# One ring of PSUM banks for projections and MLP, with squares and rotation taken from the bank and Newton steps on GpSimd

## The chip, the core and the metric

The kernel runs on one core of a Trainium2 chip. A core has TensorE (PE in the profile; its weight loads are PEld), VectorE (DVE), ScalarE (ACT), GpSimd (POOL) and SyncE (SP), which issues most DMAs. Matrix results land in eight PSUM banks of 128 partitions x 512 f32; DVE and ACT read these banks. Each engine works through its own list of instructions in program order and waits on semaphores. The metric is the device time of one execution in microseconds (us); lower is better.

## What is computed

Eight samples of 1024 tokens x 256 channels go through an attention block (first stage) and then through two layers of a local transformer. What matters here is one such layer:

```python
def _layer(x, wqkv, qs, ksc, wo, lg, lb, w1, b1, w2, b2):
    h = shift_token(x)              # half of the channels one token late
    q, k, v = jnp.split(h @ wqkv, 3, axis=-1)      # 8 heads of 64
    q = l2norm(q) * qs
    k = l2norm(k) * ksc
    q, k = rotary_xpos(q, k)        # x * cos + rotate_half(x) * sin
    o = local_attention(q, k, v)    # windows of 128, each sees itself and the one before
    x = x + o @ wo
    h = shift_token(x)
    mu = h.mean(-1, keepdims=True)
    var = h.var(-1, keepdims=True)
    h = (h - mu) / jnp.sqrt(var + 1e-05) * lg + lb
    a, g = jnp.split(h @ w1 + b1, 2, axis=-1)
    h = a * jax.nn.gelu(g, approximate=False)
    return x + h @ w2 + b2
```

## The kernel before, in words

After the modulation and the attention stage come two calls of `layer_stage`, one for each layer (names with the prefix b_ in the profile). Each runs a hardware loop over the eight samples and then a short closing part. The work of one sample is laid out in steps `pp` from -6 to 36. Scores are computed at steps 0 to 31, one pair of heads per step, so 4 steps make a window of 128 rows and 8 windows a sample. Every engine runs the same list of steps, each with its own pieces of a step in the order in which its code names them; no scheduler intervenes. Lines are those of the kernel before.

**A window's queries and keys.** Six steps ahead of a window's first scores TensorE projects its queries (L1573, 128x512, six matmuls), five ahead its keys, and at its first step its values; all three go through bank p. Matrices are kept as a high and a low part, and three products stand for one. ACT copies q and k into SBUF (`b_qk`, L1442) and squares both in one instruction; DVE sums the squares (L1732) and clips the sums (L1733); ACT seeds the inverse root by a logarithm and an exponential; DVE refines it with Newton steps (L114 `b_inv`) and scales the q part (L1759). DVE also multiplies q and k by the cosine table in one instruction (L1743, 128x1024) and by the sine table in two (L1749). GpSimd adds the halves (L1352, two instructions) and scales k by its inverse norms (L1358). TensorE turns q and k (L1606, bank t); ACT takes the high parts, DVE the low parts (`b_q_lo` L1784, `b_k_lo` L1790).

**Attention.** Per step: scores (L1620, banks s0 and s1), masked row maxima on DVE (L1775), exponentials on ACT (L1470), shares on DVE (L1795) that GpSimd multiplies in (L1367), the turn of the weights (L1632, bank et), the meeting with the values (L1645, bank ot). Once a window: the copy of the turned weights on DVE (L1802), `b_o_lo` (L1816), the output projection (L1573 into bank t) and its addition to the rows (`add_attention`).

**MLP.** Four units of 256 tokens; three have their statistics at steps 13, 21 and 29 (`plan_mlp`), the last one of a sample runs ahead of the next sample's first step (u = -1, from step -6). Per unit: row statistics on DVE (L1835), variance, the seed of its root on ACT and Newton steps on DVE (L114 `b_rstd`), the normalised rows, their turn and scaling (hT), six pieces `ag` one step after hT (TensorE 128x256, then gelu on ACT, then a multiplication by DVE, L1871), the product's low part on GpSimd (L1384), w2 and the store. hT, ag and w2 alternate between banks m0 and m1. GpSimd makes the low part of hT (L1373) and adds b2 (L1378). Before the first gelu of a unit ACT loads its table (L1495).

**What sets the order of banks.** `plan_fills` lists for each bank what fills it in which turn; a fill waits until the turn before it in the same bank has been read. Banks before: p, t, s0, s1, et, ot, m0, m1.

## Time and profile before

| | us |
|---|---|
| Three runs | 5864.05, 5875.67, 5878.0 (median 5875.67) |
| The profiled execution's own time | 5885.19 |
| Its span | 5883.4 |
| Mean granted clock of TensorE, share of full | 0.888 |

Busy time over the whole span: PE 4514.8 us (77%), weight loads 3167.8 (54%), DVE 3568.6 (61%), ACT 2631.7 (45%), POOL 1731.0 (29%). The attention stage ends at about 2040 us; the rest are the two layer stages, about 229 us for a sample of the first layer and 233 for one of the second. The page's own chain of waits is made of short pieces (15% of it is "issue", 8% POOL, 7% PE), so the page says what is busy but not what decides; the timeline of one sample does. In a timeline a row is: start, duration, engine, line, operation, output <- inputs, shapes, and in brackets the idle time before it with what ended it.

### The profile page before, as it was taken

The page shows a single profiled execution, that of the slowest core. Times are in us where ns is not written, and L with a number is a line of the kernel's source. Part 1 is how long each engine was busy: PE and PEld are TensorE (multiplying, and loading weights), DVE is VectorE, ACT ScalarE, POOL GpSimd, SP SyncE. Part 2 cuts the span into 40 slices and gives each one's busy share as a digit, 9 for nine tenths or more (in the row PEclk, how much of TensorE's full clock was granted, in tenths as well). Part 3 has the DMA queues.
Part 4 walks back from the last instruction along what each step waited for, and adds up shares of the span by engine and source line. Part 5 has one row for each costly group of instructions (what it writes and reads, how often), then busy time and mean ns, then how long its engine had stood idle before and what let it go on. Part 6 is the DMA issues. An engine that isn't in the chain of part 4 may idle for free. (4 is left out here: it accounts for less than half of the span.)

```text
span 5883.4 us, 97285 instructions
## 1 busy us (share of the span) xinstructions
PE 4514.8 (77%) x31439; PEld 3167.8 (54%) x31439; DVE 3568.6 (61%) x8906; ACT 2631.7 (45%) x5436; POOL 1731.0 (29%) x1344
## 2 busy tenths in 40 slices
PE   3778777777787577887877887857788787887886
PEld 1333433333333266666666666646666666666665
DVE  3666666656666565665755755736565575575664
ACT  1434334334343254554544544535454454454543
POOL 1010110101101133433433433424343443343443
PEclk6889898989898789999988989979899898898988
DMA  4132242242222500000000000010000000000000
GB/s 93 41 79 44 57 99 45 57 73 62 65 54 55 109 15 14 13 11 15 12 13 15 10 13 17 10 55 14 20 16 15 20 15 20 20 14 18 16 15 21
DMA packets 177374, 202.00 MB, mean 34 GB/s; under 512 B 32479, under 2 KB 131259, under 8 KB 176707
## 3 DMA queue, kind: packets, MB, share of 16 engines
q1 hardware_dynamic: 176806, 194.81, 14.2%
q8 instruction: 309, 5.06, 0.4%
q14 instruction: 259, 2.12, 0.1%
HBM read 123.12 MB, written 63.25 MB: 32 GB/s over the span
## 5 line engine op out<-in xcount | busy, mean ns | idle before, releaser
L858 DVE TENSOR_REDUCE a_mx<-a_unit 128x1 f32<-128x512 f32 (+3 forms) x1584 | 817.6, 553 | 434.6 <-PE a_unit L677 303.9
L582 ACT ACTIVATE a_e_t<-a_ring 128x1024 f32<-128x1024 f32 (+3 forms) x768 | 615.4, 810 | 957.6 <-PE a_ring L702 735.8
L1367 POOL TENSOR_TENSOR b_e<-b_e,b_share 128x512 f32<-128x512 f32 (+1 forms) x512 | 527.5, 1030 | 1293.7 <-DVE b_share L1795 1293.7
L1470 ACT ACTIVATE b_e<-b_e,b_bias 128x256 f32<-128x256 f32 (+1 forms) x1024 | 498.6, 488 | 615.1 <-DVE b_bias L1775 614.0
L673 PE MATMUL a_unit<-a_k_st,a_q_st 96*128 96x512 bf16 (+3 forms) x1584 | 535.0, 345 | 206.9 <-DVE a_mx L858 167.6
L699 PE MATMUL a_ring<-a_q_st,a_k_st 99*128 99x512 bf16 (+3 forms) x1536 | 529.4, 358 | 167.0 <-DMA a_q_st<-maxima 89.9
L1573 PE MATMUL b_bank_m<-b_h_t_hi,b_w_hi 128*128 128x256 f32 x1584 | 476.0, 301 | 94.0 <-POOL b_h_t_lo L1373 71.9
L1573 PE MATMUL b_bank_p<-b_wqkv_hi,b_turned_hi 128*128 128x512 f32 x768 | 373.6, 486 | 182.5 <-ACT b_qk L1442 140.1
L673 PEld LDWEIGHTS a_unit<-a_k_st,a_q_st 96*128 96x128 bf16 x1584 | 154.4, 100 | 598.3 <-DVE a_mx L858 473.5
L1573 PE MATMUL b_bank_m<-b_h_t_lo,b_w_hi 128*128 128x256 f32 x1584 | 461.3, 291 | 0.0
L1573 PE MATMUL b_bank_m<-b_h_t_hi,b_w_lo 128*128 128x256 f32 x1584 | 460.6, 291 | 0.0
L1871 DVE SCALAR_TENSOR_TENSOR b_ag<-b_bank_m,b_b_c,b_ag 128x256 f32<-128x256 f32 x396 | 191.5, 484 | 398.4 <-ACT b_ag L1498 393.6
L1775 DVE CUSTOM_DVE_ANT_0 b_e<-b_bank_s,b_mask,b_scale_q 128x256 f32<-128x256 f32 (+1 forms) x1024 | 432.2, 460 | 0.0
L1632 PE MATMUL b_bank_et<-b_ident,b_e 128*128 128x128 f32 x1920 | 352.5, 309 | 39.5 <-ACT b_e_t L1551 36.0
L1573 PEld LDWEIGHTS b_bank_m<-b_h_t_hi,b_w_hi 128*128 128x128 f32 x1584 | 317.9, 201 | 109.6 <-POOL b_h_t_lo L1373 77.9
L1498 ACT ACTIVATE b_ag<-b_bank_m,b_b_c 128x256 f32<-128x256 f32 x396 | 187.8, 474 | 402.7 <-PE b_bank_m L1573 400.2
L514 POOL TENSOR_TENSOR a_x<-a_x,a_xl 128x1024 f32<-128x1024 f32 x16 | 37.7, 2355 | 1084.6 <-DVE a_xl L962 1084.6
L1645 PE MATMUL b_bank_ot<-b_e_t,b_v 128*64 128x128 f32 x3840 | 356.2, 306 | 0.0
L718 PE MATMUL a_outp<-a_e_t,a_v_t 128*32 128x512 f32 (+3 forms) x3072 | 352.8, 533 | 0.0
L1620 PE MATMUL b_bank_s<-b_k_hi,b_q_hi 64*128 64x256 f32 (+1 forms) x1024 | 204.5, 390 | 176.1 <-DVE b_bias L1775 121.6
L699 PEld LDWEIGHTS a_ring<-a_q_st,a_k_st 99*128 99x128 bf16 x1536 | 160.0, 104 | 328.3 <-issue 264.2
L1573 PE MATMUL b_bank_p<-b_wqkv_hi,b_turned_lo 128*128 128x512 f32 x768 | 336.4, 438 | 0.0
(217 smaller groups left out, 11767.5 us busy)
## 6 DMA issues: line engine op xcount, KB each, us to landing
a_q_st<-parts_q SPq DMA_DIRECT2D x216, 128.0 KB, 7.3
a_k_st<-parts_k SPq DMA_DIRECT2D x216, 128.0 KB, 9.7
b_fl<-f_rows SPq DMA_DIRECT2D x72, 256.0 KB, 4.0
parts_q<-a_qk_part SPq DMA_DIRECT2D x18, 768.0 KB, 3.5
parts_k<-a_qk_part SPq DMA_DIRECT2D x18, 768.0 KB, 3.8
a_xl<-in_L_attn_x SPq DMA_DIRECT2D x9, 1024.0 KB, 8.9
f_rows<-b_fr SPq DMA_DIRECT2D x33, 256.0 KB, 2.1
b_x_l<-x_rows SPq DMA_DIRECT2D x33, 256.0 KB, 3.1
```

The source lines that it names most:

```text
L582: act.activation(e_t[:, step % 2, 2 * pair:2 * pair + 2, 0:cols], slot[:, :].rearrange("p (h t) -> p h t", h=2)[:, :, 0:cols], ACT.Exp).th ...
L673: mm = pe.matmul(slot[:, 0:cols], q_st[0:KROWS, head, t * P:(t + 1) * P], k_st[0:KROWS, head, 512 * piece:512 * piece + cols], start=True, ...
L699: mm = pe.matmul(slot[:, 512 * hh:512 * hh + cols], k_st[:, head, s * P:(s + 1) * P], q_st[:, head, lo:lo + cols], start=True, stop=not di ...
L718: mm = pe.matmul(outp[32 * h:32 * h + VW, lo:512], v_t[:, s, 4 * g + h, :], e_t[:, (g * NSTEP + n) % 2, h, 0:512 - lo], start=(s == 0), st ...
L858: dve.reduce_max(mx[:, h, col:col + 1], slot[:, 0:cols], AX.X).then_inc(read.sem, 1)
L1367: pool.tensor_tensor(weights, weights, share[:, pp, :].unsqueeze(2) .broadcast_to([P, 2, 2 * WIN - lo]), ALU.mult).then_inc(e_done.sem, 1)
L1470: ins = act.activation(weights, weights, ACT.Exp, scale=-1.0, bias=bias[:, pp, hh:hh + 1], accum_out=total[:, pp, hh:hh + 1])
L1573: mm = pe.matmul(out, lhs(a), rhs(b), start=(first and j == 0), stop=(last and j == 2))
L1620: mm = pe.matmul(slot[:, lo:2 * WIN], q_p[a][rows, w % 2, p, :], k_p[b][rows, p, key_slots(w), :], start=(j == 0), stop=(j == 2))
L1632: mm = pe.transpose(slot[:, at:at + WIN], e[:, pp % E_RING, hh, b * WIN:(b + 1) * WIN], ident[:, :])
L1645: mm = pe.matmul(bank["ot"][D2 * hh:D2 * (hh + 1), p * WIN:(p + 1) * WIN], v[:, u % 3, 2 * p + hh, :], e_t[:, pp % 2, 2 * hh + b, :], star ...
L1775: dve.tensor_tensor_reduce(out=e[:, pp % E_RING, hh, lo:], in0=src[:, lo:2 * WIN], in1=mask[:, int(w > 0 and w % K_RING == 0), lo:], scale ...
```

## The change

The two banks m0 and m1 and the bank p become a ring of three, r0 to r2, in which q, k, v, hT, ag and w2 follow one another in the order of the steps. v is projected one step later (step 1 of the window), w2 of every unit at s + 6 (before: s + 5, and s + 6 for u = -1). Queries are turned at step -3 (before -2), keys at -2 (before -1). For the closing part, where there are no projections, `CLOSING_AT` counts the fills apart.

ACT squares q and k straight from the ring's bank, in two instructions of 128x512 with one operand in PSUM, and copies neither. DVE multiplies by cosine and sine straight from the bank (L1800 and L1805 of the kernel after, 128x512 each, four per window): q's two in the last step of a window, k's two in the first step of the next, where k's are interleaved with the MLP's first multiplications. The bank comes free with the sine product. The clip of the sums, the Newton steps for the norms and for the variance, the q scale and the addition of eps go to GpSimd, as tensor operations on 128x16 and 128x2 with the constants in a small tile; factors of one half are folded into `ln_g` and the q scale, so a Newton step is four instructions. ACT's seed of the inverse root now waits for GpSimd's clip (`clipped`) and stands behind the exponentials of the step; DVE waits for `scale_done` before a window's first row maxima (`scores_met`).

```diff
+CONSTS = (3.0, -QK_SCALE / 4, LN_EPS)
...
-        put(s + 5 + int(u < 0), "w2", u, None)
+        put(s + 6, "w2", u, None)
...
+PROJECTED_AT = (("q", -6), ("k", -5), ("v", 1))
+TURNED_AT = (("qT", -3), ("kT", -2))
+
+
+def window_at(pp, step):
+    w, p = divmod(pp - step, PAIRS)
+    return w if p == 0 and 0 <= w < NWIN else None
...
-    slots = {name: [] for name in ("p", "t", "s0", "s1", "et", "ot", "m0", "m1")}
-    n_m = 0
+    slots = {name: [] for name in ("t", "s0", "s1", "et", "ot", "r0", "r1", "r2")}
+    n_r = 0
+
+    def ring(fill):
+        nonlocal n_r
+        slots[f"r{n_r % 3}"].append(fill)
...
-        for what, step in (("q", -6), ("k", -5), ("v", 0)):
+        for what, step in PROJECTED_AT:
             if (pp - step) % PAIRS == 0 and 0 <= (pp - step) // PAIRS < NWIN:
-                slots["p"].append((what, (pp - step) // PAIRS))
-        if pp % PAIRS == PAIRS - 1 and 0 <= (pp + 1) // PAIRS < NWIN:
-            slots["t"].append(("kT", (pp + 1) // PAIRS))
-        if pp % PAIRS == 2 and 0 <= (pp + 2) // PAIRS < NWIN:
-            slots["t"].append(("qT", (pp + 2) // PAIRS))
+                ring((what, (pp - step) // PAIRS))
+        for what, step in TURNED_AT:
+            if (pp - step) % PAIRS == 0 and 0 <= (pp - step) // PAIRS < NWIN:
+                slots["t"].append((what, (pp - step) // PAIRS))
...
-                slots[f"m{n_m % 2}"].append((piece, u, m))
-                n_m += 1
+                ring((piece, u, m))
...
-        qk = sb("qk", [P, 2, H2, D2])
+        sq = sb("sq", [P, 2, H2, D2])
         rot = sb("rot", [P, 2, H2, D2])
-        sq = rot[:, :, :, :].rearrange("p a h d -> p (a h) d")
...
-                def rotate(w):
-
-                    pool.wait_ge(turned_parts.sem, turned_parts.at(i, w + 1))
-                    for a in range(2):
-                        pool.tensor_tensor(qk_rot[:, a, :, :], qk_rot[:, a, :, :], rot[:, a, :, :], ALU.add)\
-                            .then_inc(summed_parts.sem, 1)
+                spot = CLOSING_AT if closing else FILL_AT
+                pool_steps.start(pool, i)
+                step = pool_steps.step
+
+                def rotate(what, w):
+
+                    name, n, _ = FILL_AT[(what, w)]
+                    pool.wait_ge(read[name].sem, read[name].at(i, n + 1))
+                    a = int(what == "k")
+                    pool.tensor_tensor(qk_rot[:, a, :, :], qk_rot[:, a, :, :], rot[:, a, :, :], ALU.add)\
+                        .then_inc(summed_parts.sem, 1)
+
+                def clip_sums(w):
+                    pool.wait_ge(summed.sem, summed.at(i, w + 1))
+                    pool.sem_inc(sums_seen.sem, 1)
+                    pool.tensor_scalar(sums[:, w, :], sums[:, w, :], NORM_MIN ** 2, None, ALU.max)\
+                        .then_inc(clipped.sem, 1)
+
+                def newton(y, v, tmp):
+                    step(pool.tensor_tensor(tmp, y, y, ALU.mult))
+                    step(pool.tensor_tensor(tmp, tmp, v, ALU.mult))
+                    step(pool.tensor_tensor(tmp, const(3.0, tmp.shape[-1]), tmp, ALU.subtract))
+                    return pool.tensor_tensor(y, y, tmp, ALU.mult)
+
+                def inverse_norms(w):
+                    pool.wait_ge(inv_seeded.sem, inv_seeded.at(i, w + 1))
+                    step(newton(inv[:, w, :], sums[:, w, :], inv_tmp[:, :]))
+                    pool.tensor_tensor(scale_q[:, w, :], inv[:, w, 0:H2], const(-QK_SCALE / 4, H2), ALU.mult)\
+                        .then_inc(scale_done.sem, 1)
 
                 def scale_k(w):
                     pool.wait_ge(summed_parts.sem, summed_parts.at(i, 2 * w + 2))
-                    pool.wait_ge(inv_done.sem, inv_done.at(i, w + 1))
                     pool.tensor_tensor(qk_rot[:, 1, :, :], qk_rot[:, 1, :, :],
...
-                    if piece == "hT":
+                    if piece == "moments":
+                        pool.wait_ge(aggr_done.sem, aggr_done.at(i, u + 2))
+                        pool.tensor_tensor(var[:, :], aggr[:, :, 1], const(LN_EPS, UNIT), ALU.add)\
+                            .then_inc(var_done.sem, 1)
+                    elif piece == "norm":
+                        pool.wait_ge(rstd_seeded.sem, rstd_seeded.at(i, u + 2))
+                        newton(rstd[:, :], var[:, :], var_tmp[:, :]).then_inc(rstd_done.sem, 1)
+                    elif piece == "hT":
...
-                        if pp % PAIRS == 1 and (pp + 3) // PAIRS < NWIN:
-                            rotate((pp + 3) // PAIRS)
-                        if pp % PAIRS == 2 and 0 <= (pp + 2) // PAIRS < NWIN:
-                            scale_k((pp + 2) // PAIRS)
+                        w = window_at(pp, -4)
+                        if w is not None:
+                            rotate("q", w)
+                            clip_sums(w)
+                        w = window_at(pp, -3)
+                        if w is not None:
+                            rotate("k", w)
+                            inverse_norms(w)
...
+            act.mul(ln_g[:, :], ln_g[:, :], 0.5).then_inc(hi_split, 1)
...
-                def square(w):
-                    _, n, _ = FILL_AT[("k", w)]
-                    act.wait_ge(read["p"].sem, read["p"].at(i, n + 1))
+                def square(what, w):
+                    src, _ = wait_full((what, w))
                     if w:
-                        act.wait_ge(summed_parts.sem, summed_parts.at(i, 2 * w))
-                    act.activation(sq.rearrange("p h d -> p (h d)"),
-                                   qk[:, :, :, :].rearrange("p a h d -> p (a h d)"), ACT.Square)\
+                        act.wait_ge(summed.sem, summed.at(i, w))
+                    act.activation(sq[:, int(what == "k"), :, :].rearrange("p h d -> p (h d)"), src[:, :], ACT.Square)\
                         .then_inc(squared.sem, 1)
 
...
-                        if pp % PAIRS == 0 and (pp + 4) // PAIRS < NWIN:
-                            w = (pp + 4) // PAIRS
-                            inverse_root(summed, w + 1, inv_seeded, inv[:, w, :], sums[:, w, :], logs[:, :])
                         if 0 <= pp - MEET_LAG < NPP and (pp - MEET_LAG) % PAIRS == PAIRS - 1:
                             values_hi((pp - MEET_LAG) // PAIRS)
-                        if pp % PAIRS == 3 and 0 <= (pp + 1) // PAIRS < NWIN:
-                            take_k((pp + 1) // PAIRS)
-                        if pp % PAIRS == 3 and (pp + 5) // PAIRS < NWIN:
-                            square((pp + 5) // PAIRS)
+                        if window_at(pp, -3) is not None:
+                            take_q(window_at(pp, -3))
+                        if window_at(pp, -2) is not None:
+                            take_k(window_at(pp, -2))
+                        w = window_at(pp, -4)
+                        if w is not None:
+                            inverse_root(clipped, w + 1, inv_seeded, inv[:, w, :], sums[:, w, :], logs[:, :])
...
                 def sum_squares(w):
-                    dve.wait_ge(squared.sem, squared.at(i, w + 1))
-                    step(dve.reduce_sum(sums[:, w, :], sq, AX.X))
-                    dve.tensor_scalar(sums[:, w, :], sums[:, w, :], NORM_MIN ** 2, None, ALU.max)\
+                    dve.wait_ge(squared.sem, squared.at(i, 2 * w + 2))
+                    dve.reduce_sum(sums[:, w, :], sq[:, :, :, :].rearrange("p a h d -> p (a h) d"), AX.X)\
                        .then_inc(summed.sem, 1)
 
...
+                    a = int(what == "k")
+                    src, back = wait_full((what, w))
+                    dve.wait_ge(squared.sem, squared.at(i, 2 * w + a + 1))
+
+                    name, _, k = FILL_AT[(what + "T", w - 1)] if w else FILL_AT[("fT", 0, 1)]
                     dve.wait_ge(full[name].sem, full[name].at(i, k + 1))
-                    cos = tab[:, :, 0, w, :].unsqueeze(2).broadcast_to([P, 2, H2, D2])
-                    dve.tensor_tensor(qk_rot[:, :, :, :], qk[:, :, :, :], cos, ALU.mult)
+                    x = src[:, :].rearrange("p (h d) -> p h d", h=H2)
+                    cos = tab[:, a, 0, w, :].unsqueeze(1).broadcast_to([P, H2, D2])
+                    dve.tensor_tensor(qk_rot[:, a, :, :], x, cos, ALU.mult)
                     beside(0)
...
+                    x = src[:, :].rearrange("p (h r d) -> p h r d", h=H2, r=2)[:, :, ::-1, :]
+                    sin = tab[:, a, 1, w, :].rearrange("p (r d) -> p r d", r=2).unsqueeze(1)\
+                        .broadcast_to([P, H2, 2, D2 // 2])
+                    dve.tensor_tensor(rot[:, a, :, :].rearrange("p h (r d) -> p h r d", r=2), x, sin, ALU.mult)\
+                       .then_inc(back, 1)
+                    beside(1)
 
                 def scores_met(pp):
                     if pp >= E_RING:
 
                         _, _, k = FILL_AT[("et", pp - E_RING)]
                         dve.wait_ge(full["et"].sem, full["et"].at(i, k + 1))
...
-                        if pp % PAIRS == 0 and (pp + 4) // PAIRS < NWIN:
-                            sum_squares((pp + 4) // PAIRS)
-                            rotation_products((pp + 4) // PAIRS, lambda n: activated(pp, n, n + 1))
+                        w = window_at(pp, -5)
+                        if w is not None:
+                            rotation_products("q", w)
+                        w = window_at(pp, -4)
+                        if w is not None:
+                            sum_squares(w)
+                            rotation_products("k", w, lambda n: activated(pp, n, n + 1))
+                            activated(pp, 2, 3)
                         else:
                             activated(pp, 0, 3)
-                        if pp % PAIRS == 1 and (pp + 3) // PAIRS < NWIN:
-                            inverse_norms((pp + 3) // PAIRS)
                     activated(pp, 3, HK)
...
-                        if pp % PAIRS == 3 and 0 <= (pp + 1) // PAIRS < NWIN:
-                            key_lo((pp + 1) // PAIRS)
+                        if window_at(pp, -3) is not None:
+                            query_lo(window_at(pp, -3))
+                        if window_at(pp, -2) is not None:
+                            key_lo(window_at(pp, -2))
```

How the order moves, in three places. On GpSimd, at the window's first step with an MLP unit's hT (step 15 into 16), before; `b_qk_rot` L1352 is the addition of the rotated halves, `b_e` L1367 the shares of one step:

```order
L1373 TENSOR_TENSOR b_h_t_lo<-b_h_scaled,b_h_t_hi 128x512
L1378 TENSOR_TENSOR b_fr<-b_fr,b_b_r 128x512
L1365 REGISTER_ALU
L1367 TENSOR_TENSOR b_e<-b_e,b_share 128x512
L1365 REGISTER_ALU
L1367 TENSOR_TENSOR b_e<-b_e,b_share 128x512
L1350 REGISTER_ALU
L1352 TENSOR_TENSOR b_qk_rot<-b_qk_rot,b_rot 128x512 x2
```

The same place after, with the following step:

```order
L1430 TENSOR_TENSOR b_h_t_lo<-b_h_scaled,b_h_t_hi 128x512
L1435 TENSOR_TENSOR b_fr<-b_fr,b_b_r 128x512
L1415 REGISTER_ALU
L1417 TENSOR_TENSOR b_e<-b_e,b_share 128x512
L1383 REGISTER_ALU
L1385 TENSOR_TENSOR b_qk_rot<-b_qk_rot,b_rot 128x512
L1389 REGISTER_ALU
L1391 TENSOR_SCALAR b_sums<-b_sums 128x16
L1415 REGISTER_ALU
L1417 TENSOR_TENSOR b_e<-b_e,b_share 128x512
L1383 REGISTER_ALU
L1385 TENSOR_TENSOR b_qk_rot<-b_qk_rot,b_rot 128x512
```

q's addition stands one step earlier, k's apart from it, and the clip of the sums stands behind hT's low part, b2, a share and q's addition. On DVE, at step 16, before; `b_ag` L1871 is the multiplication of one MLP piece:

```order
L1731 REGISTER_ALU
L1732 TENSOR_REDUCE b_sums<-b_rot 128x16
L97 REGISTER_ALU
L1733 TENSOR_SCALAR b_sums<-b_sums 128x16
L1738 REGISTER_ALU
L1743 TENSOR_TENSOR b_qk_rot<-b_qk,b_tab 128x1024
L1871 SCALAR_TENSOR_TENSOR b_ag<-b_bank_m,b_b_c,b_ag 128x256
L1749 TENSOR_TENSOR b_rot<-b_qk,b_tab 128x512
```

and after:

```order
L1787 REGISTER_ALU
L1788 TENSOR_REDUCE b_sums<-b_sq 128x16
L1783 REGISTER_ALU
L1800 TENSOR_TENSOR b_qk_rot<-b_bank_r,b_tab 128x512
L1919 SCALAR_TENSOR_TENSOR b_ag<-b_bank_r,b_b_c,b_ag 128x256
L1805 TENSOR_TENSOR b_rot<-b_bank_r,b_tab 128x512
L1783 REGISTER_ALU
L1919 SCALAR_TENSOR_TENSOR b_ag<-b_bank_r,b_b_c,b_ag 128x256
```

The sine product of k, which frees its bank of the ring, stands behind the first MLP multiplication, as the sine product of q did in SBUF. On DVE at the last step of a window, before:

```order
L1727 REGISTER_ALU
L1802 COPY b_e_t<-b_bank_et 128x512
L1816 TENSOR_TENSOR b_o_lo<-b_bank_ot,b_o_hi 128x512
L1727 REGISTER_ALU
L1790 TENSOR_TENSOR b_k_lo<-b_bank_t,b_k_hi 128x4x128
```

and after:

```order
L1783 REGISTER_ALU
L1794 REGISTER_ALU
L1800 TENSOR_TENSOR b_qk_rot<-b_bank_r,b_tab 128x512
L1805 TENSOR_TENSOR b_rot<-b_bank_r,b_tab 128x512
L1783 REGISTER_ALU
L1852 COPY b_e_t<-b_bank_et 128x512
L1866 TENSOR_TENSOR b_o_lo<-b_bank_ot,b_o_hi 128x512
```

q's two products stand ahead of the copy of the turned weights and of the low part of the output, and k's low part has left this step.

In the ring, around the first unit: ... k5 r2, hT0 r0, ag0 r1, ag1 r2, ag2 r0, ag3 r1, ag4 r2, ag5 r0, v4 r1, q6 r2, k6 r0, w2 r1. So the second piece of a unit's ag follows the keys k5 in their bank. At step 24 it is the same with k7; at step 32 and ahead of step 0 no keys stand there.

## Rows read from the trace of the kernel before

**Rows 1.** Busy time per engine in two samples, one of each layer (windows).
```profile
3213.71:3442.26 228.55, 185.98 (x1320) 149.23 (x1321) 142.12 (x373) 114.81 (x280) 86.17 (x72) 0.91 0.04 13
4903.42:5138.38 234.96, 191.36 (x1320) 153.83 (x1321) 142.13 (x373) 115.50 (x280) 94.16 (x80) 0.88 0.06 17
```

**Rows 2.** What TensorE waited for in the layer stages: us in total, times, longest.
```profile
PE b_bank_p L1573 <- ACT b_qk L1442: 140.1, 80, 3.6
...
PE b_bank_t L1606 <- POOL b_qk_rot L1352: 98.7, 112, 2.9
```

**Rows 3.** Groups of DVE instructions in the layer stages: busy us, mean ns | idle before.
```profile
L114 DVE SCALAR_TENSOR_TENSOR b_inv<-b_inv_tmp,b_inv 128x16 f32<-128x16 f32 x128 | 136.2, 1064 | 4.4
...
L1784 DVE TENSOR_TENSOR b_q_lo<-b_bank_t,b_q_hi 128x512 fp32r<-128x512 f32 x128 | 88.1, 689 | 62.0 <-ACT b_q_hi L1447 62.0
...
L114 DVE SCALAR_TENSOR_TENSOR b_rstd<-b_var_tmp,b_rstd 128x2 f32<-128x2 f32 x66 | 10.6, 161 | 2.3
```

**Rows 4.** The same view of GpSimd: the attention stage's sizes.
```profile
L514 POOL TENSOR_TENSOR a_x<-a_x,a_xl 128x1024 f32<-128x1024 f32 x16 | 37.7, 2355 | 1084.6 <-DVE a_xl L962 1084.6
...
L504 POOL TENSOR_TENSOR a_gate_bp<-a_modb,a_b_p 128x256 f32<-128x256 f32 x8 | 5.8, 723 | 201.7 <-DMA a_x<-in_L_attn_x 201.7
```

**Rows 5.** GpSimd's groups in the layer stages: two chained instructions' second, smallest fill.
```profile
L1397 POOL TENSOR_TENSOR b_fr<-b_fr,b_x_l 128x512 f32<-128x512 f32 x33 | 42.5, 1287 | 2.6
...
L1316 POOL MEMSET b_b_c<- 128x12 f32 x2 | 0.2, 108 | 0.0
```

**Rows 6.** Timeline of one window of layer 0 (start us, us, engine, line).
```profile
3050.23 0.39 PE L1620 MATMUL b_bank_s<-b_k_hi,b_q_hi 64*128 64x256 f32 x2 [0.67 <-DVE b_k_lo L1790]
...
3051.96 0.39 PE L1573 MATMUL b_bank_t<-b_wo_hi,b_o_hi 128*128 128x256 f32 x1
...
3053.57 0.39 PE L1620 MATMUL b_bank_s<-b_k_hi,b_q_hi 64*128 64x256 f32 x2
...
3057.16 2.50 POOL L1352 TENSOR_TENSOR b_qk_rot<-b_qk_rot,b_rot 128x512 f32<-128x512 f32 x2
...
3060.11 0.50 PE L1573 MATMUL b_bank_p<-b_wqkv_hi,b_turned_hi 128*128 128x512 f32 x1
3060.21 0.17 DVE L1795 RECIPROCAL b_share<-b_total 128x2 f32<-128x2 f32 x1 [0.31 <-DVE b_scale_q L1759]
...
3061.10 0.69 DVE L1784 TENSOR_TENSOR b_q_lo<-b_bank_t,b_q_hi 128x512 fp32r<-128x512 f32 x1
...
3061.46 1.04 POOL L1358 TENSOR_TENSOR b_qk_rot<-b_qk_rot,b_inv 128x512 f32<-128x512 f32 x1
...
3061.70 0.39 PE L1620 MATMUL b_bank_s<-b_k_hi,b_q_hi 64*128 64x256 f32 x2
...
3066.18 0.39 PE L1620 MATMUL b_bank_s<-b_k_hi,b_q_hi 64*128 64x256 f32 x2 [0.50 <-DVE b_k_lo L1790]
```

**Rows 7.** The timeline further on: the next two windows, with one MLP unit.
```profile
3077.11 0.29 DVE L1835 BATCH_NORM_STATS2 b_stats<-b_fr 128x6 f32<-128x128 f32 x1 [1.24 <-DMA b_hs<-b_fr]
...
3086.75 0.38 PE L1620 MATMUL b_bank_s<-b_k_hi,b_q_hi 64*128 64x256 f32 x2
...
3088.05 1.29 POOL L1373 TENSOR_TENSOR b_h_t_lo<-b_h_scaled,b_h_t_hi 128x512 fp32r<-128x512 f32 x1 [4.38 <-ACT b_h_t_hi L1492]
...
3091.16 1.28 ACT L1495 ACT_TABLE_LOAD   x1
...
3099.60 0.39 PE L1620 MATMUL b_bank_s<-b_k_hi,b_q_hi 64*128 64x256 f32 x2
...
3117.97 0.39 PE L1620 MATMUL b_bank_s<-b_k_hi,b_q_hi 64*128 64x256 f32 x2 [0.69 <-DVE b_k_lo L1790]
```

**Rows 8.** Windows around an idle stretch of TensorE; PEclk is the granted clock.
```profile
3176.38:3180.66 4.28, 0.00 (x0) 0.03 (x1) 2.43 (x14) 0.92 (x5) 0.87 (x1) 0.92 0.11 35
3180.66:3186.84 6.18, 6.08 (x35) 4.46 (x35) 4.85 (x17) 3.33 (x11) 1.21 (x2) 0.50 0.00 0
```

**Rows 9.** Timeline of a sample's last output projection.
```profile
3209.51 0.39 PE L1573 MATMUL b_bank_t<-b_wo_hi,b_o_hi 128*128 128x256 f32 x1 [1.43 <-DVE b_o_lo L1816]
```

126 lines of the change are left out of this document (58 added, 68 removed).

## The prediction

> **What bounds the kernel now.** The page gives shares; none of its engines is full. I read next the windows of two whole samples [rows 1]: 228.55 us in layer 0 with TensorE busy 185.98, 234.96 in layer 1 with 191.36. Four fifths is TensorE, the rest its waits, so a sample is a chain of TensorE work and of stalls. Then TensorE's waits [rows 2]: the projections wait for ACT's copies of q and k 140.1 us in all (80 times), the turns of q and k for GpSimd's additions 98.7 us (112 times). Over 16 samples that is 8.8 and 6.2 us a sample, and just these the change goes at. Last the timeline, to see what ends each stretch. A window without MLP work runs from its first scores at 3050.23 to the next at 3066.18: 15.95 us [rows 6]. The stretch with an MLP unit, from scores 12 to scores 20, runs from 3066.18 to 3117.97: 51.8 us [rows 6, 7]. I forecast by walking such stretches with the new order and the old durations.
>
> **Part 1, removed waits in a plain window.** The copies of q and k leave ACT, and q and k are turned a step earlier. But the window is held by a second chain just as long. Follow it: in its last step DVE does the shares and row maxima (0.89, from the reciprocal at 3060.21 to the next instruction at 3061.10 [rows 6]), then, new, q's cosine and sine from the bank, 2 x 0.69 (priced as a 512-wide product with one PSUM operand, 0.689 [rows 3]), then the copy of the turned weights, 0.69 by the same row: 2.9. Only that copy frees bank et, and TensorE's next turn and meeting come behind it. Scores, turn and meeting together take 1.73 (3050.23 to 3051.96 [rows 6]); I give 1.2 of it to turn and meeting. Then the output projection, 1.61 (3051.96 to 3053.57), v's projection, 1.59 (a projection from 3060.11 to 3061.70 [rows 6]), and scores and their first maxima, 0.7. Up to here 8.0. Then the GpSimd chain for the keys: one addition 1.25 (half of the 2.50 for two), a share 1.04 (512 wide, as the scaling), five chained small steps 1.5 (next part), the scaling 1.04 [rows 6], gaps 0.3: 5.1. Then the turn 0.5 (estimate: four transposes), k's projection 1.6 and scores 0.7: 2.8. Sum 15.9 against 15.95. **Removed waits are replaced: -0.1 a window**, bounds -1.5 (DVE's products hidden) to +1.
>
> **Part 2, small steps on GpSimd.** No small tensor operation of GpSimd is in the trace. Its two fitted sizes, 128x1024 at 2355 ns and 128x256 at 723 ns [rows 4], give 2.125 ns an element and 0.18 us fixed, so 0.21 for 16 elements. The gap between two chained instructions is 2.6/33 = 0.08 us [rows 5]. Five chained: 5 x 0.29 = 1.5. Bounds: the smallest fill took 108 ns [rows 5], which gives 5 x 0.19 = 0.9; DVE's own Newton steps of 128x2 took 161 ns [rows 3], and twice that with the gap, 0.40, gives 2.0; the shortest tensor operation in a row, 723 ns, gives 4.0. I take 1.5, the fit, since its two rows are the same operation. Five stand on the path of a window, eight windows to a sample, so each 0.1 us is worth up to 4 a sample.
>
> That DVE loses its Newton steps is worth something: 128 of them of 128x16 took 1064 ns on average, against 161 for 128x2 [rows 3], since they ran beside GpSimd's additions. The Trainium skill, "SBUF — State Buffer", section on the two sides, tells of a port pair that DVE and GpSimd share and that one of them holds alone; the trace agrees, 1064 against 161 ns. By that page the new products with one operand in PSUM would not be held up. But in the plain window these 2.1 us lay off the path, so I count no gain beyond the walk.
>
> **Part 3, an MLP unit inside a window (steps 12 to 20).** Before 51.8 us: scores 12 at 3066.18, 16 at 3086.75, 17 at 3099.60, 20 at 3117.97 [rows 6, 7], so 20.6, 12.85 and 18.4.
> - *12 to 16.* The unit's statistics wait for the DMA of the shifted rows until 10.9 after scores 12 (3077.11 [rows 7]). From there: statistics and aggregation 1.3, row maxima 0.9, seeds, square and copies on ACT with DVE's low keys behind them 4.1 (an estimate, three 512-wide copies and three short steps), normalised rows, 1.1, with the maxima's last part inside: 10.9 + 1.3 + 0.9 + 4.1 + 1.1 is 18.3, taken 18.4, **-2.2**. Eps and four small GpSimd steps for the variance are in it, 5 x 0.29 in place of DVE's own.
> - *16 to 17.* This is where I expect the loss. In the ring the second piece of ag (ag1) follows k5 in bank r2, and DVE frees that bank with k's sine product, which its order puts behind the first MLP multiplication. That one waits for ACT's first gelu, which waits for the table load 1.28 [rows 7]; ACT's order has the inverse root of k's norms ahead of it, and that now waits for GpSimd's clip. GpSimd has ahead of the clip: hT's low part 1.29 [rows 7], the addition of b2 1.29 (as the 512-wide addition of [rows 5]), a share 1.04 and q's addition 1.25 [rows 6]. In numbers from scores 16: DVE done with step 15 at 3.5, hT's high part 4.1, low part 5.5, b2 6.8, share and addition 9.1, clip 9.4, logarithm and exponential 9.9, table 11.1, gelu 11.7, multiplication 12.1, sine product 12.8. So ag1 starts at 12.8, where ag0 ended at 6.9 (low part at 5.5, one piece 1.4): TensorE stands 5.9 us. Then five ag at 1.44, 7.2, and v 1.59. A piece's 1.44 is an estimate: of the 12.85 between scores 16 and 17 I take off 1.73 for scores to meeting, 1.61 for the output projection and 0.9 for hT's turn, and six pieces share the rest. Besides, the clock: after an idle stretch of 4.28 us TensorE ran 6.18 us at a granted clock of 0.50, that is 1.2 GHz instead of 2.4 [rows 8]. The same behind the new stall would cost at most half of such a stretch, 3.1; I take 2.6. Scores 17 at 12.8 + 7.2 + 2.6 + 1.6 = 24.2, **+11.35**.
> - *17 to 20.* Scores 0.7, GpSimd's key chain 5.2, turn 0.5, projections of q 1.6, weights and values 1.7, w2 4.3, which now stands a step later and no longer waits for the product's low part: 14.0 against 18.4, **-4.4**.
>
> Together 56.6 against 51.8: +4.8. The unit at 21 to 27 has the same stall (ag1 behind k7), but its path through steps 20 to 24 was less bound by DVE; I walked it to 53.7, +1.9 (bounds 0 to +4.8). The units at 32 and ahead of step 0 have no keys before ag1 in the ring.
>
> **Part 4, the rest of a sample.** Lead and first eight steps: v is later and no ACT copies stand before the first scores: -1.4 (bounds -3 to +2). Steps 28 to 31: the values' projection hides in the wait for the rows' DMA: 0. Tail: the last output projection waited 1.43 for its low part [rows 9], which now stands ahead of w2, and 0.66 of the meeting before it goes: -2.1. Five plain windows' worth is in the -0.1.
>
> **Sum.** +4.8 + 1.9 - 0.1 - 1.4 + 0 - 2.1 = +3.1 a sample, 16 samples: +50. The profiled execution took 5885.19 us (span 5883.4 and 1.8 around it), so 5935; the median of the runs is 5875.67, 9.5 below it, so **5925**.
>
> **Rivals.**
> - *Faster: no clock loss and cheap small steps.* If TensorE keeps its full clock behind the stall, 2 x 2.6 = 5.2 a sample go, and the sum is -2.1; small steps at the fill's 108 ns take another 3. For it: a sample's mean granted clock is 0.91 [rows 1] though it has a fifth of waits, so not every stall costs clock. It gives 5876 - 16 x 2.1 = 5842, with both 5795. It decides as soon as the stall in the middle falls under 3 us. Against: [rows 8]. Chance 0.22.
> - *Slower still: GpSimd's small steps cost 0.35 or more.* Then the key chain grows 0.7 a window in part 1's path and delays the clip and the seeds too: +3.5 a sample, 5925 + 56 = 5980; at the 723 ns row over 6100. For it: the shortest row; against: the fit. Chance 0.12. The Trainium skill, "GPSIMD Engine Reference", section 4.1, gives elementwise work to VectorE and says that GpSimd is about twice as slow with two inputs; by that page a step is 2 x 161 ns, this rival's case. No row here shows it for such small tiles.
> - *Same: the stall and the removed waits cancel.* ag1 stands only 3 us and the plain window gains 0.5: 5876. Chance 0.14.
> - The change doing other than it says is not among them: the order of each engine shows it done.
> - My forecast, part 3's stall as walked: chance 0.52, its own range 5895 to 5960.
>
> **Numbers.** A measurement of this kernel tells 0.3% (17.6 us) from no change. Faster by more 0.24 (the first rival and a little of the others), same 0.17, slower 0.59. The range 5840 to 5990 takes in the fast rival's first price and the slow one's, and leaves out both of their far ends.
>
> **What the profile after would show.** For part 3: TensorE waiting for DVE's sine product at ag1, near 6 us, 32 times, the granted clock at half behind it, and ACT's logarithm waiting for GpSimd's clip. For part 1: plain windows of 15.9 us, TensorE's waits for ACT's copies gone, and a wait of 2 to 3 us for the copy of the turned weights in its place; k's turn waiting for GpSimd's scaling. For part 2: small steps of 0.21 us. For part 4: a tail of 31 us instead of 33. The forecast is wrong if the clip comes before 6 us after scores 16, or if a plain window is shorter than 15 us; in the second case 16 x 4 windows at each 1 us are 64 us.

## The result, and the profile after

| | before | after |
|---|---|---|
| Median of the runs, us | 5876.84 (4 runs, 5864.05 to 5880.5) | 5938.98 (4 runs, 5933.19 to 5944.98) |
| Profiled execution: own time, span, us | 5885.19, 5883.4 | 5944.98, 5943.2 |
| Mean granted clock | 0.888 | 0.874 |

The kernel after takes 1.0103 times as long, 95% interval 1.0091 to 1.0116: 62 us slower, where 49 were forecast (5925 against 5875.67). The time lies in the range and on the forecast side. The busy time of DVE fell by 512 us (3568.6 to 3056.4), ACT's by 115, and GpSimd's rose by 195 (1731.0 to 1925.6); the span rose all the same.

Windows of the kernel after, two whole samples, one of each layer, the counterpart of [rows 1] (columns as there: span of the window, busy time of PE, PEld, DVE, ACT and POOL, granted clock, DMA share, GB/s):

```profile
3224.64:3453.77 229.13, 187.28 (x1320) 152.41 (x1321) 110.53 (x325) 107.63 (x272) 97.46 (x140) 0.90 0.04 13
4941.60:5177.99 236.39, 190.81 (x1321) 155.10 (x1321) 110.53 (x325) 107.46 (x272) 107.85 (x149) 0.88 0.06 17
```

DVE is busy 110.5 us where it was 142.1, and the samples are longer (229.13 against 228.55, 236.39 against 234.96). TensorE has the same instructions; its waits were exchanged. The waits of TensorE in the layer stages (us in all, times, longest), to be read against [rows 2]:

```profile
PE b_bank_r L1631 <- DVE b_rot L1805: 136.2, 32, 5.5
PE b_bank_t L1664 <- POOL b_qk_rot L1408: 106.1, 112, 3.5
PE b_bank_r L1723 <- DVE b_hn L1898: 98.2, 50, 12.7
...
PE b_bank_et L1690 <- DVE b_e_t L1852: 78.3, 80, 1.1
```

The 140.1 us for ACT's `b_qk` are gone. By stretches they stood in steps 12 to 16 (3.5 us a sample), in 20 to 24 (3.6) and in the lead (1.7), none of them in a plain window. In 12 to 16 and 20 to 24 TensorE now waits 1.3 and 1.1 us for the normalised rows (`b_hn`, 98.2 us in 50 times, before 22.6 in 9). The new large wait is the one for the sine product of k, 136.2 us in only 32 waits: 4.3 us each, two in every sample. The turn of the keys waits as much as before (106.1 against 98.7 us, 112 times both), now for GpSimd's scaling.

Walking the starts of the scores through both traces, as the forecast did, gives this ("16 to 17" is from the start of the scores of step 16 to that of step 17, "scores 16" for short; the lead runs from a sample's first turn to its scores 0, the tail from scores 31 to the next sample; us per sample, mean of 12 samples, six of each layer, the first and last of a layer left out; worked out from the timeline):

| stretch | before | after | difference | forecast |
|---|---|---|---|---|
| lead and steps 0 to 8 | 65.5 | 65.8 | +0.3 | -1.4 |
| steps 8 to 12, the plain window | 16.0 | 16.2 | +0.2 | -0.1 |
| 12 to 16 | 21.0 | 18.5 | -2.5 | -2.2 |
| 16 to 17 | 12.85 | 23.3 | +10.5 | +11.35 |
| 17 to 20 | 18.3 | 14.0 | -4.4 | -4.4 |
| 20 to 28, the second unit | 52.0 | 53.7 | +1.7 | +1.9 |
| 28 to 31 | 11.8 | 12.25 | +0.5 | 0 |
| tail | 33.2 | 30.6 | -2.6 | -2.1 |
| sum | | | +3.7 | +3.1 |

One part of this is only bookkeeping. A v projection, 1.6 us of TensorE, stood in 17 to 20 and now stands in 16 to 17; another went from 25 to 28 into 24 to 25, and one left the lead for 28 to 31. So of the +10.5 some 8.9 are a loss, and of the -4.4 some 2.8 a gain. Another part is the clock. Before the change TensorE stood 3.43 us in the middle of 12 to 16, waiting for ACT's copy, and 1.4 us later the granted clock fell to 0.50 for 3.4 us; the stretch has 0.91 in the mean. After it the stretch has 1.00, and TensorE is busy 14.9 us there for the same instructions instead of 16.5: more than half of the -2.5.

The timeline of the kernel after at one such unit, from scores 16 to scores 17 (start, us, engine; in brackets the idle time before):

```profile
3091.76 0.39 PE L1678 MATMUL b_bank_s<-b_k_hi,b_q_hi 64*128 64x256 f32 x2 [0.23 <-DVE b_bias L1825]
...
3100.38 0.25 POOL L1391 TENSOR_SCALAR b_sums<-b_sums 128x16 f32<-128x16 f32 x1
3100.67 0.21 ACT L1534 ACTIVATE b_logs<-b_sums 128x16 f32<-128x16 f32 x1 [3.17 <-POOL b_sums L1391]
...
3101.15 1.28 ACT L1553 ACT_TABLE_LOAD   x1
3102.44 0.47 ACT L1556 ACTIVATE b_ag<-b_bank_r,b_b_c 128x256 f32<-128x256 f32 x1
3103.05 0.48 DVE L1919 SCALAR_TENSOR_TENSOR b_ag<-b_bank_r,b_b_c,b_ag 128x256 f32<-128x256 f32 x1 [5.02 <-ACT b_ag L1556]
3103.45 0.68 DVE L1805 TENSOR_TENSOR b_rot<-b_bank_r,b_tab 128x512 f32<-128x512 f32 x1
3104.18 0.29 PEld L1631 LDWEIGHTS b_bank_r<-b_h_t_hi,b_w_hi 128*128 128x128 f32 x1 [4.03 <-DVE b_rot L1805]
...
3115.21 0.19 PEld L1678 LDWEIGHTS b_bank_s<-b_k_hi,b_q_hi 64*128 64x128 f32 x2 [0.36 <-issue]
```

Read it as a chain. GpSimd clips the sums only at 8.6 us after scores 16, 2.95 us after DVE had them ready, and ACT had waited 3.17 us for that with its logarithm; then seed, table load, gelu, DVE's multiplication, and behind it the sine product. 0.05 us after that product TensorE, idle for 3.83 us, starts ag1. And the windows of the same stretch (the third number from the end is the granted clock):

```profile
3091.76:3100.35 8.59, 7.50 (x42) 6.44 (x42) 5.85 (x13) 3.27 (x10) 4.88 (x5) 0.60 0.01 2
3100.35:3104.18 3.83, 0.00 (x1) 0.00 (x0) 1.08 (x2) 2.19 (x4) 0.28 (x2) 0.82 0.00 0
3104.18:3110.00 5.82, 5.82 (x29) 5.82 (x30) 0.48 (x1) 0.77 (x2) 0.00 (x0) 0.54 0.00 0
3110.00:3115.21 5.21, 5.21 (x41) 4.67 (x39) 1.94 (x4) 2.40 (x5) 0.00 (x0) 1.00 0.01 3
```

After 3.83 us of standing TensorE works 5.82 us at a granted clock of 0.54, near the lower of its two levels (1.2 GHz), and then at 1.00 (2.4 GHz). The 0.60 of the first row is such a stretch too. From 3089.40 on TensorE stood 1.48 us (for the normalised rows), 0.23 and 1.09 us (for the copy of the turned weights) with little work between:

```profile
3089.40:3093.47 4.07, 1.27 (x11) 0.87 (x11) 4.07 (x14) 1.57 (x5) 1.04 (x1) 0.88 0.01 2
3093.47:3098.50 5.03, 5.03 (x25) 4.37 (x26) 4.14 (x10) 2.21 (x6) 2.85 (x3) 0.50 0.02 3
```

The new work on GpSimd and DVE, groups of the layer stages (busy us, mean ns | idle before):

```profile
L1391 POOL TENSOR_SCALAR b_sums<-b_sums 128x16 f32<-128x16 f32 x128 | 31.6, 247 | 23.6 <-DVE b_sums L1788 23.6
L1397 POOL TENSOR_TENSOR b_inv_tmp<-b_consts,b_inv_tmp 128x16 f32<-128x16 f32 x128 | 28.6, 223 | 10.0
...
L1398 POOL TENSOR_TENSOR b_rstd<-b_rstd,b_var_tmp 128x2 f32<-128x2 f32 x66 | 13.0, 196 | 5.3 <-POOL b_var_tmp L1397 0.2
```

```profile
L1800 DVE TENSOR_TENSOR b_qk_rot<-b_bank_r,b_tab 128x512 f32<-128x512 f32 x256 | 174.6, 682 | 0.0
L1805 DVE TENSOR_TENSOR b_rot<-b_bank_r,b_tab 128x512 f32<-128x512 f32 x256 | 173.9, 679 | 0.0
```

A small tensor operation of GpSimd costs 196 to 197 ns with 2 elements and 218 to 223 with 16; the gap between two chained ones is 10.0/128 = 0.08 us. DVE's products from the bank take 682 and 679 ns.

### The profile page after: what moved, and what is told of

Read it like the earlier page. It is cut to its first block and busy times, and to the rows that moved or that the text cites. A ratio compares the mean times of both kernels' runs of the same rounds, so it can differ in the third digit from the quotient of the medians.

```text
span 5943.2 us, 98473 instructions
## 1 busy us (share of the span) xinstructions
PE 4556.7 (77%) x31439; PEld 3229.1 (54%) x31439; DVE 3056.4 (51%) x8130; ACT 2516.5 (42%) x5310; POOL 1925.6 (32%) x2448
## 3 DMA queue, kind: packets, MB, share of 16 engines
q1 hardware_dynamic: 176806, 194.81, 13.9%
## 5 line engine op out<-in xcount | busy, mean ns | idle before, releaser
L1631 PE MATMUL b_bank_r<-b_h_t_hi,b_w_hi 128*128 128x256 f32 x1584 | 508.1, 321 | 203.0 <-DVE b_rot L1805 136.2
L1919 DVE SCALAR_TENSOR_TENSOR b_ag<-b_bank_r,b_b_c,b_ag 128x256 f32<-128x256 f32 x396 | 191.6, 484 | 718.2 <-ACT b_ag L1556 718.2
L1631 PE MATMUL b_bank_r<-b_h_t_lo,b_w_hi 128*128 128x256 f32 x1584 | 494.8, 312 | 0.0
L1631 PE MATMUL b_bank_r<-b_h_t_hi,b_w_lo 128*128 128x256 f32 x1584 | 491.1, 310 | 0.0
L1631 PEld LDWEIGHTS b_bank_r<-b_h_t_hi,b_w_hi 128*128 128x128 f32 x1584 | 357.1, 225 | 218.4 <-issue 132.2
L1690 PE MATMUL b_bank_et<-b_ident,b_e 128*128 128x128 f32 x1920 | 350.5, 306 | 138.2 <-DVE b_e_t L1852 78.3
L1556 ACT ACTIVATE b_ag<-b_bank_r,b_b_c 128x256 f32<-128x256 f32 x396 | 188.3, 475 | 510.1 <-PE b_bank_r L1631 509.7
L1631 PE MATMUL b_bank_r<-b_wqkv_hi,b_turned_hi 128*128 128x512 f32 x768 | 344.2, 448 | 47.6 <-DVE b_turned_lo L1861 47.6
L1631 PEld LDWEIGHTS b_bank_r<-b_h_t_lo,b_w_hi 128*128 128x128 f32 x1584 | 356.2, 225 | 0.0
L1631 PEld LDWEIGHTS b_bank_r<-b_h_t_hi,b_w_lo 128*128 128x128 f32 x1584 | 352.5, 223 | 0.0
L1441 POOL TENSOR_TENSOR b_hid_lo<-b_ag,b_hid_hi 128x768 fp32r<-128x768 f32 x132 | 238.6, 1830 | 338.1 <-ACT b_hid_hi L1564 338.1
```

What stands on the lines that cost most here:

```text
L1441: pool.tensor_tensor(hid_p[1][:, ms, :], ag[:, ms, 0, :], hid_p[0][:, ms, :].bitcast(F32), ALU.subtract).then_inc(hid_lo.sem, 1)
L1631: mm = pe.matmul(out, lhs(a), rhs(b), start=(first and j == 0), stop=(last and j == 2))
L1690: mm = pe.transpose(slot[:, at:at + WIN], e[:, pp % E_RING, hh, b * WIN:(b + 1) * WIN], ident[:, :])
```

## Experiments: the stall at the MLP unit

The theory: the change's loss sits in one chain of four links, clip behind GpSimd's queue, seed before the table load, sine product behind the first multiplication, ag1 in k's bank. The first experiment cuts the third link, the second the first. Links two and four are read from the order and from the releasers in the trace; no run cuts them.

**e_sine** (kernel after, one order changed):

```diff
-    rotation_products("k", w, lambda n: activated(pp, n, n + 1))
-    activated(pp, 2, 3)
+    rotation_products("k", w)
+    activated(pp, 0, 3)
```

> Kernel after, with one order changed on DVE: at a window's first step k's sine product stands ahead of the first MLP multiplication instead of behind it, so k's bank of the ring comes free before gelu. Theory A (the ring: ag1 waits in k's bank for that product): the 3.8 us stall ahead of ag1 goes, the granted clock behind it stays up, scores 16 to 17 fall from 23.4 to about 17.8 us (what is left is ag3 waiting 0.4 for the first multiplication), likewise 24 to 25: 32 x 5.5 = 176 us, 5763 us. Rival B (the late first gelu paces the pieces in any order): 16 to 17 stays above 21 us, 5860 or more.

Measured: 5762.21 us (ratio to before 0.9818, 0.9797 to 0.9838), 177 us below the kernel after. The timeline of e_sine at the same unit:

```profile
3040.55 0.39 PE L1678 MATMUL b_bank_s<-b_k_hi,b_q_hi 64*128 64x256 f32 x2 [0.23 <-DVE b_bias L1825]
...
3046.74 0.68 DVE L1805 TENSOR_TENSOR b_rot<-b_bank_r,b_tab 128x512 f32<-128x512 f32 x1
...
3052.47 0.35 PE L1631 MATMUL b_bank_r<-b_h_t_hi,b_w_hi 128*128 128x256 f32 x1 [0.54 <-DVE b_ag L1919]
...
3058.24 0.39 PE L1678 MATMUL b_bank_s<-b_k_hi,b_q_hi 64*128 64x256 f32 x2
```

The sine product starts 6.2 us after scores 16 and ag1 and ag2 follow ag0 without a pause; what is left is a wait of 0.54 us ahead of ag3, for DVE's first multiplication, as theory A has it. 16 to 17 takes 17.69 us (mean of both layers; 17.8 expected), 24 to 25 takes 17.6. The clock:

```profile
3040.55:3049.00 8.45, 7.37 (x43) 6.49 (x44) 6.46 (x14) 3.26 (x10) 4.74 (x5) 0.60 0.01 2
3049.00:3058.20 9.20, 8.66 (x68) 7.98 (x66) 2.72 (x6) 5.11 (x10) 0.42 (x2) 1.00 0.00 0
```

The first part has a granted clock of 0.60 as in the kernel after (0.60), behind the same small waits; behind it TensorE stays at 1.00. So the half clock behind the stall belongs to the stall, the one ahead of it does not. It is a good part of what is left: 17.7 us against 12.85 before, of which 1.6 are v.

**e_clip** (kernel after, clip on DVE):

```diff
-    dve.reduce_sum(sums[:, w, :], ...).then_inc(summed.sem, 1)
+    step(dve.reduce_sum(sums[:, w, :], ...))
+    dve.tensor_scalar(sums[:, w, :], sums[:, w, :], NORM_MIN ** 2, None, ALU.max)\
+       .then_inc(summed.sem, 1)
...
-    inverse_root(clipped, w + 1, ...)
+    inverse_root(summed, w + 1, ...)
```

(Besides, GpSimd's clip and its two semaphores are removed.)

> Kernel after, with the clip of the sums back on DVE behind its reduction; ACT's seeds wait for DVE alone and GpSimd has no clip. The order of k's sine product stays. Theory A with its GpSimd link (the clip queues behind hT's low part, b2, a share and q's addition): logarithm 3 us earlier at the two units, stall ahead of ag1 from 3.8 to 0.7 us, with the clock 4.5 us a unit: 32 x 4.5 = 144, 5795 us. If GpSimd's queue is not a link of the chain: no change, 5939.

Measured: 5833.46 us (0.9938, 0.9922 to 0.9955), 106 us less than the kernel after, not 144. Timeline and windows of e_clip from scores 16 (3064.31) on:

```profile
3070.80 0.21 ACT L1525 ACTIVATE b_logs<-b_sums 128x16 f32<-128x16 f32 x1 [0.75 <-DVE b_sums L1780]
...
3073.02 0.47 ACT L1547 ACTIVATE b_ag<-b_bank_r,b_b_c 128x256 f32<-128x256 f32 x1 [0.46 <-PE b_bank_r L1622]
...
3074.76 0.19 PEld L1622 LDWEIGHTS b_bank_r<-b_h_t_hi,b_w_hi 128*128 128x128 f32 x1 [1.98 <-DVE b_rot L1797]
```

```profile
3064.31:3072.00 7.69, 6.60 (x36) 5.74 (x37) 6.60 (x14) 4.41 (x13) 3.98 (x5) 0.56 0.01 2
3072.00:3078.00 6.00, 4.22 (x26) 4.02 (x26) 1.35 (x3) 1.51 (x3) 0.96 (x1) 0.78 0.00 0
3078.00:3084.91 6.91, 6.91 (x51) 6.37 (x51) 2.14 (x5) 2.70 (x5) 0.00 (x0) 0.94 0.01 2
```

The logarithm starts 6.5 us after scores 16 instead of 8.9, so GpSimd's queue is a link. But the first gelu could then not start before ag0's matmuls were done (ACT waited 0.46 us for them), and the stall is 1.78 us, where I had 0.7. Even behind this shorter stall the clock is not full: 0.78 and 0.94 in the two windows that hold it and what follows. 16 to 17 takes 20.4 against 18.9 expected.

**e_both** has both edits.

> Both edits: k's sine product first and the clip on DVE. Theory A: the two take away the same stall, so they do not add up; 16 to 17 about 17 us, 5740 us, at most 30 below the better of the two. Theory B (two separate costs): the sum of both gains, near 5620 us.

Measured: 5720.55 us (0.9743, 0.9727 to 0.9759). That is 42 us below e_sine, where at most 30 were expected, and far from the 5656 that the two gains give together (5939 - 177 - 106; the expectation's "near 5620" was too low a sum). So the two edits meet in the same stall, and theory B falls; 16 to 17 takes 16.7, 24 to 25 takes 16.4. Against e_sine the two stretches give 2.2 us a sample, 36 of the 42 us. TensorE stands there nearly as long (1.8 and 2.5 us against 1.9 and 2.7), but its mean granted clock is 0.90 and 0.99 against 0.84 and 0.92.

## Experiments: the key chain and the Newton steps

**e_more** (kernel after; five chained multiplications of 128x16 into a scratch tile added on GpSimd, nothing left out):

```diff
     step(newton(inv[:, w, :], sums[:, w, :], inv_tmp[:, :]))
+    for _ in range(5):
+        step(pool.tensor_tensor(inv_tmp[:, :], inv[:, w, :], inv[:, w, :], ALU.mult))
```

> Kernel after, with five more chained 128x16 multiplications on GpSimd for each window, between its Newton steps and the q scale; they write a scratch tile and change nothing. They cost 5 x 0.30 = 1.5 us a window on GpSimd. If GpSimd's key chain (addition, Newton, scaling, turn) sets the plain windows, as the forecast had it: most windows grow by 1.5, 128 windows, +130 to +190 us, 6070 to 6130. If it lies beside other work: within 20 us of 5939.

Measured: 6136.86 us, 198 more than the kernel after (128 windows x 1.5 = 192). TensorE's waits in e_more:

```profile
PE b_bank_t L1666 <- POOL b_qk_rot L1410: 271.2, 112, 5.0
PE b_bank_r L1633 <- DVE b_rot L1807: 164.1, 32, 5.5
```

The wait for the scaling grew from 106.1 to 271.2 us in 112 turns, 1.47 us each: the added time arrives whole at TensorE. The wait for the sine product grew by 28 us besides. GpSimd's chain of addition, Newton and scaling is on the path of almost every window.

**f_newton** (e_both, with the norms' Newton steps and q's scale back on DVE):

```diff
+    def inverse_norms(w):
+        dve.wait_ge(inv_seeded.sem, inv_seeded.at(i, w + 1))
+        y, tmp = inv[:, w, :], inv_tmp[:, :]
+        step(dve.tensor_tensor(tmp, y, y, ALU.mult))
+        step(dve.scalar_tensor_tensor(out=tmp, in0=tmp, scalar=-1.0, in1=sums[:, w, :], ...))
+        step(dve.scalar_tensor_tensor(out=y, in0=tmp, scalar=3.0, in1=y, ...))
+        dve.tensor_scalar(scale_q[:, w, :], inv[:, w, 0:H2], -QK_SCALE / 4, None, ALU.mult)\
+           .then_inc(scale_done.sem, 1)
```

(DVE does this at a window's step -3, behind that step's row maxima and first multiplications; GpSimd's scaling of k waits for `scale_done`.)

> The kernel with both edits (k's sine product first, clip on DVE; 5720.55 us), and the norms' Newton steps and the q scale back on DVE, as three steps of 128x16 and one of 128x8; GpSimd keeps the variance's. Theory A (the key chain addition, Newton, scaling runs one after the other on GpSimd, 1.25 + 1.5 + 1.04, and is on the path of plain windows): DVE's steps run beside GpSimd's addition, at up to 1.2 us each while it lasts and 0.2 behind it, so the chain is some 0.9 us shorter in about 100 windows: 5630 us. Rival (DVE's steps beside GpSimd cost 1.2 each throughout and hold the shares and maxima queued behind them): slower, 5790 us or more. If the Newton steps' place does not matter: 5720.

Measured: 5673.7 us (0.9659, 0.9643 to 0.9675), 47 less than e_both: the direction of theory A, half its size. DVE's second and third step in f_newton (shortest/median/longest in ns, first and last start):

```profile
L1802 DVE SCALAR_TENSOR_TENSOR b_inv_tmp<-b_inv_tmp,b_sums x128: 174/1214/1226, 2094.2 to 5574.5; 128x16 f32<-128x16 f32 x128
...
L1804 DVE SCALAR_TENSOR_TENSOR b_inv<-b_inv_tmp,b_inv x128: 174/176/1190, 2094.4 to 5575.7; 128x16 f32<-128x16 f32 x128
```

TensorE's wait for GpSimd's scaling, 104.7 us in 112 times in e_both, became:

```profile
PE b_bank_t L1652 <- POOL b_qk_rot L1397: 51.9, 48, 2.6
```

The second step takes 1.2 us in the 104 windows in which it meets GpSimd's addition, and 175 ns in the 16 in which nothing of GpSimd runs beside it (8 more meet a share). The third takes 175 ns in 120 windows and 1.19 us in the 8 in which it meets the addition: only what runs beside GpSimd's operation is dear, and it takes as long as that operation. The 1064 ns of [rows 3] is such a mean, 104 times 1.2 us and 16 times 175 ns among them. The chain so got 53 us shorter at the turn, and 47 of them reached the end.

**g_newton** (kernel after with this edit alone):

> Kernel after, with nothing changed but the norms' Newton steps and q scale back on DVE (clip and k's sine product stay where the change put them). In the kernel with the other two edits this gave 47 us. Theory A (the Newton chain on GpSimd is a second, separate loss of the change, in the plain windows): the same 47 here, 5892 us, the two stretches 16 to 17 and 24 to 25 unchanged at 23 us. Rival (the two losses share a cause): under 15 us.

Measured: 5869.2 us (0.9987, 0.9974 to 0.9999), 70 us less than the kernel after, where 47 were expected:

```profile
PE b_bank_r L1628 <- DVE b_rot L1802: 150.1, 32, 5.5
...
PE b_bank_t L1661 <- POOL b_qk_rot L1405: 51.5, 48, 2.6
```

The stall for the sine product stays (150.1 against 136.2 us), the wait for the scaling halves (51.5 against 106.1). The two losses are separate. Why it is 70 here and 47 behind the other edits is open; by stretches the difference is in 8 to 12 (-0.5 us a sample here, -0.1 there) and in 16 to 17 (-0.6 and -0.2, the granted clock up from 0.72 to 0.78 here).

## Experiments: the moves in the steps

All three start from e_both (5720.55 us) and undo one move of the change.

**f_turns** (`TURNED_AT = (("qT", -2), ("kT", -1))`):

> The kernel with both edits, and the turns of q and k back at steps -2 and -1 (as before the change). Theory A: TensorE's waits for GpSimd's scaling (105 us in 112 turns of k) shrink since the turn comes a step later, but DVE's low keys become the last thing ahead of the next window's first scores (51 us in all before the change): net -50, 5670 us. Rival (the turned step is what the change needs): slower than 5720 by over 20.

Measured: 5799.07 us (0.987, 0.9853 to 0.9886), 79 more. Theory A falls, its sign was wrong; the rival holds.

```profile
PE b_bank_s L1669 <- DVE b_k_lo L1832: 249.9, 96, 3.4
```

The wait for the scaling went, and one of 249.9 us in 96 times for DVE's low keys came, 2.6 us each, ahead of the scores: a turn at the window's end leaves no time for ACT's copy and DVE's low part. The lengthened stretches are 8 to 12 (19.0 against 15.8), 12 to 16 and 20 to 24 (about +2 and +3) and the lead (+2.5); steps 0 to 4 are 3.3 us shorter and 16 to 17 1.5.

**f_v0** (`("v", 0)`):

> The kernel with both edits, and v projected at a window's first step instead of its second. The change lost 4.3 us a sample in steps 0 to 4 and won 2.0 in the lead. Theory A (v's 1.6 us only changed sides of the first scores): lead +1.6, steps 0 to 4 -1.6, sum the same, 5720 +- 15. Rival (v at step 1 is what costs there, standing with w2 on the path): 3 us a sample less, 5670 us.

Measured: 5793.71 us (0.9864, 0.9848 to 0.9881), 73 more. For lead and steps 0 to 4 theory A is right (47.6 and 53.5 us in the two layers against 47.9 and 53.2): the lead takes 1.2 us more and steps 0 to 4 take 1.2 less. But that gives back only 1.2 of the 4.3 us that steps 0 to 4 lost by the change. The rest is other waits and clock: there are three projections in these steps before and after, TensorE stands 4.6 us in them instead of 2.3 (2.9 of it for GpSimd's scaling), and its mean granted clock is 0.85 instead of 0.95. For the whole sample the theory is wrong:

```profile
PE b_bank_t L1655 <- POOL b_qk_rot L1400: 178.5, 112, 4.9
```

The turn of k waits 178.5 us instead of 104.7, and the wait for the sine products grows from 18.3 us in 24 times to 66.7 in 64. With v ahead of the scores, the stretches that hold an MLP unit and the one behind it are longer (12 to 16 +1.8, 17 to 20 +2.4, 20 to 24 +3.7, 25 to 28 +2.7), while 16 to 17 and 24 to 25, which v left, are 3 shorter.

**f_w2** (w2 at s + 5 for the units at 13, 21 and 29):

> The kernel with both edits, and w2 of the units at 13, 21 and 29 back at s + 5. The forecast gave the gain of 4.4 us in steps 17 to 20 (and the like in 25 to 28) to w2 no longer waiting for the product's low part on GpSimd. Theory A: that wait comes back, 1.5 to 3 us a unit, 48 units, 5790 to 5860 us. Rival (the gain is from the other moves): within 20 us of 5720.

Measured: 5874.33 us (1.0001, 0.9991 to 1.0011), 154 more. Theory A's direction, and above its 5860.

```profile
PE b_bank_r L1622 <- POOL b_hid_lo L1433: 100.5, 98, 4.7
```

The wait for the product's low part is 100.5 us instead of 33.8, and it explains less than half of the 154. The stretches show where the rest is: the tail 35.4 against 30.7, 25 to 28 15.6 against 13.1, 17 to 20 15.9 against 13.9, 20 to 24 18.8 against 17.6. In the tail TensorE waits 1.7 us a sample for the low part of the output and 1.5 for the product's, where e_both has 0.2 of the first, and the mean granted clock is 0.81 against 0.88. So w2's later step gave the tail and 2.0 of the 4.4 us in steps 17 to 20.

## Experiments: towards a faster version

From f_newton (5673.7 us). **g_et** puts q's two products behind the copy of the turned weights on DVE, **g_b2** moves GpSimd's addition of b2 from hT's step to behind the product's low part, **g_all** does both:

```diff
-    w = window_at(pp, -5)
-    if w is not None:
-        rotation_products("q", w)
...
     if 0 <= pp - TURN_LAG < NPP and pp % 4 == 3:
         take_turned(pp - TURN_LAG)
+    w = window_at(pp, -5)
+    if w is not None:
+        rotation_products("q", w)
```

> The fastest so far (both edits and Newton on DVE, 5673.7 us), with q's cosine and sine products behind DVE's copy of the turned weights instead of ahead of it. TensorE waits 69.6 us in 80 times for that copy (0.87 each; the forecast put 1.4 us of products into a plain window's path). Theory A (the copy is on the path): these waits go and 40 to 70 us with them, 5605 to 5635 us. Rival (TensorE then waits for ACT's or DVE's next piece instead, the low part of the output and q's bank): within 15 us of 5674, or slower.

> The same kernel of 5673.7 us, with GpSimd's addition of b2 moved from hT's step to behind the product's low part. It takes 1.28 us out of GpSimd's queue ahead of a share and q's addition at steps 15, 23, 31. With the clip on DVE it is no longer ahead of gelu. Theory A (it was a link only through the clip): within 10 us of 5674. Rival (the shares queued behind it hold TensorE's turn of the weights): 1.3 us in 48 units, 60 us less, 5614.

> The kernel of 5673.7 us with both of these moves (q's products behind the copy, b2 behind the product). Theory A: the gain of the first alone, 5605 to 5635 us. If both rivals hold, 5614 us by b2 alone.

Measured: g_et 5652.81 us (0.9623, 0.9599 to 0.9647), g_b2 5670.06 (0.9659, 0.9639 to 0.968), g_all 5651.09 (0.9616, 0.9599 to 0.9633). g_b2 is f_newton again, as theory A has it: with the clip on DVE the b2 addition is no link. That it was one through the clip is read from GpSimd's order; no run moves it with the clip still on GpSimd. g_et's 21 us less are half of the least that was expected, and its interval still touches f_newton's. Its waits tell where the rest went:

```profile
PE b_bank_t L1652 <- POOL b_qk_rot L1397: 62.3, 47, 2.6
...
PE b_bank_ot L1691 <- DVE b_o_lo L1865: 47.4, 43, 1.2
```

The wait for the copy (69.6 us in f_newton) is off the list, but TensorE now waits 47.4 us for the low part of the output, which stands behind q's products, and 62.3 instead of 51.9 for the scaling. The fastest version is g_all, within the noise of g_et: all moves of the change kept but three (sine product first, clip and norms' Newton steps on DVE), plus these two, 0.9616 of the kernel before.

## Why the prediction was right, point by point

**The stall (part 3), the step that decides: right in mechanism and near in size.** The chain came as walked: gelu at 10.7 us after scores 16 (forecast 11.1), sine product done at 12.4 (12.8), scores 17 at 23.45 (24.2) in the timeline shown. e_sine and e_clip show two of the four links by cutting them. The stall itself was over-sized: 3.83 us (4.3 in the mean of all 32) instead of 5.9, because ag0 ended at 8.6 and not at 6.9. hT's low part was ready at 5.2, but TensorE came to ag0 only at 6.5: it had waited 1.09 us for the copy of the turned weights, and the stretch ran at a granted clock of 0.60, which the forecast had at full. This changed nothing in the sum, since the sine product's time sets the start of ag1. The clock's loss behind the stall, taken as 2.6, is 5.82 x 0.46 = 2.7 by its row; [rows 8] was a fair price.

**17 to 20, 12 to 16 and the second unit: right in size** (-4.4, -2.5 and +1.7), the reasons only in part. The reason given for -4.4, w2 that no longer waits, carries about half: TensorE waited 1.8 us a sample for the product's low part there before, and f_w2 gives 2.0 back. Another 1.6 is v's projection, which left the stretch for 16 to 17. For 12 to 16 the forecast walked the path of the statistics; it did not speak of the clock, which is more than half of the -2.5.

**The plain window (part 1): right link by link, wrong in what TensorE waits for.** One plain window of the kernel after, with scores 8 at 2593.97 and scores 12 at 2609.58:

```profile
2592.85 0.17 DVE L1845 RECIPROCAL b_share<-b_total 128x2 f32<-128x2 f32 x1 [0.66 <-PE b_bank_s L1678]
...
2594.94 0.68 DVE L1852 COPY b_e_t<-b_bank_et 128x512 f32<-128x512 f32 x1
...
2595.68 0.66 PE L1690 MATMUL b_bank_et<-b_ident,b_e 128*128 128x128 f32 x4 [1.09 <-DVE b_e_t L1852]
...
2600.95 1.04 POOL L1417 TENSOR_TENSOR b_e<-b_e,b_share 128x512 f32<-128x512 f32 x1 [2.08 <-DVE b_share L1845]
...
2604.56 1.04 POOL L1408 TENSOR_TENSOR b_qk_rot<-b_qk_rot,b_inv 128x512 f32<-128x512 f32 x1
...
2608.46 0.17 DVE L1845 RECIPROCAL b_share<-b_total 128x2 f32<-128x2 f32 x1 [0.59 <-PE b_bank_s L1678]
```

From the last step's shares to the end of the copy it takes 2.8 us (forecast 2.9), to GpSimd's share 8.1 (8.0), from there to the end of the scaling 4.65 (5.1), to the next window's counterpart of the start 2.9 (2.8): 15.6 us for 15.9. But the wait for the copy of the turned weights, forecast as 2 to 3 us, is 78.3/80 = 0.98 in the mean: DVE starts its 2.8 us ahead of the window's first scores, and TensorE has a turn, a meeting and these scores to do meanwhile. The waits for ACT's copies, which the part set out to replace, never stood in a plain window; what stood there before were 0.8 us for GpSimd's addition and 0.8 for DVE's low keys. TensorE's idle time there hardly changed (1.5 and 1.4 us). The +0.2 is clock: 0.96 in the mean of steps 8 to 12 against 1.00. The sum takes the -0.1 once, although it speaks of five plain windows; that is 0.4 us a sample, 6 us in all.

**Small steps (part 2): right.** The fit from the two large sizes gave 0.21 us and 0.08 of gap; 0.22 and 0.08 were measured. The 161 ns of DVE's 128x2 step, doubled, would have been too much, and the 723 ns row far too much. For DVE's lost Newton steps I counted no gain and no loss; g_newton and f_newton show that, within the new order, these steps on GpSimd cost 47 to 70 us more than on DVE. This is not a term of the sum that was missing, since the walk had the 1.5 us in the chain, but the forecast did not say that the same steps on DVE, half beside the addition, were cheaper for the path.

The Trainium skill ("GPSIMD Engine Reference", section 4.1) puts GpSimd at about twice DVE's time for two-input elementwise work. Here a 128x2 step takes 197 ns against 161, and a 128x16 step 223 against DVE's 175 with nothing of GpSimd beside it, a factor of 1.2 to 1.3; at these sizes no run shows the factor of two. The same section's rule to give such work to DVE agrees with g_newton all the same, for a reason of order.

The Trainium skill, "SBUF — State Buffer", section "SBUF: two separate sides", tells of a port pair that one of the two engines holds for a whole instruction; of DVE's instructions it names those with two SBUF inputs, against a GpSimd operation that reads SBUF. The trace agrees, 1.2 us beside GpSimd's addition and 175 ns alone. It agrees for the products too. Here are the sine products of the kernel before, with both operands in SBUF, and those of the kernel after, with one in PSUM:

```profile
L1749 DVE TENSOR_TENSOR b_rot<-b_qk,b_tab x256: 681/684/1768, 2086.6 to 5771.8; 128x512 f32<-128x512 f32 x128
...
L1805 DVE TENSOR_TENSOR b_rot<-b_bank_r,b_tab x256: 676/679/685, 2079.7 to 5824.8; 128x512 f32<-128x512 f32 x128
```

Before, 32 of the 256 met a GpSimd operation and took 1.75 to 1.77 us; after, none took over 0.69 us, whatever GpSimd did beside it. So the forecast read the Trainium skill rightly here.

**Lead and steps 0 to 8 (part 4): mis-sized**, +0.3 for -1.4, within its bounds. Layer 0 gave -1.2, layer 1 +1.75, since there the lead hardly shortened. The first statistics of the two leads in the kernel after:

```profile
2996.75 0.29 DVE L1885 BATCH_NORM_STATS2 b_stats<-b_fr 128x6 f32<-128x128 f32 x1 [1.21 <-DMA b_hs<-b_fr]
...
4948.66 0.29 DVE L1885 BATCH_NORM_STATS2 b_stats<-b_fr 128x6 f32<-128x128 f32 x1 [4.17 <-DMA b_hs<-b_fr]
```

In layer 0 (lead from 2992.93) they start 3.8 us into the lead; in layer 1 (lead from 4941.60) 7.1, after 4.17 us of waiting for the DMA of the shifted rows. The forecast priced one lead for both layers. It also did not see that steps 0 to 4 would lose 4.3 us (waits and clock, see f_v0) while the lead won 2.0 and steps 4 to 8 another 2.0. And in 28 to 31 the moved projection does not hide whole: +0.5 for 0.

**The tail: right** (-2.6 for -2.1), and f_w2 shows the cause: w2 back at its old step, the tail is 35.4 us and the wait for the low part of the output, 1.4 us a sample before the change and 0.3 after it, is back with 1.7.

**The sum: close, in part by luck.** The lead with steps 0 to 8 came out 1.7 us a sample above its term, 27 us in all; the other terms together came out 1.05 below theirs, most of that in 16 to 17 (-0.85), and so 3.7 stands against 3.1.

**The rivals.** The faster one asked for no clock loss and cheap small steps; both conditions failed, at a granted clock of 0.54 and at 0.22 us. It was to decide as soon as the stall fell under 3 us; e_clip has 1.78 us and still reads 0.78 around it. The slower one asked for small steps of 0.35. "Same" asked for a stall of 3 us: with 3.83 in the timeline shown and 4.3 in the mean it came closer than its price shows, but the clock's part stood with it.

## What to carry to other kernels

When a buffer joins a ring, follow for each fill who frees the one before it and what stands ahead of that instruction on its engine: here one multiplication in the wrong place cost 177 us of 5939. A step that is cheap on an idle engine is dear when its queue holds longer work that must come first (the clip, 0.25 us, stood behind 4.9 us of GpSimd work and came 2.95 us after its input was ready), and steps that ran beside another engine's work can lengthen a chain when they are put behind it. A walk through the timeline with the new order, stretch by stretch, found the sum and the place; shares of busy time (DVE down by 512 us) would have told the opposite.

## What the runs showed of the hardware

- GpSimd's tensor operation of 128 x n with both operands full follows one line from 2 to 1024 elements, 0.18 us and 2.1 ns an element, within 15 ns: 197 ns (2), 223 (16), 723 (256), 1.28 us (512), 2355 (1024).
- A DVE step of 128x16 with its operands in SBUF takes 1.2 us beside GpSimd's addition and 175 ns with nothing beside it. A 128x512 product with both operands in SBUF took 684 ns, and 1.75 to 1.77 us in the 32 of 256 that met a GpSimd operation; with one operand in PSUM it took 675 to 690 ns in all 512, GpSimd's additions and shares beside many of them.
- TensorE's granted clock read 0.54 for 5.8 us behind 3.8 us of idleness and 1.00 after an edit that kept it at work. It read 0.50 for 5.0 us also behind three waits of 1.48, 0.23 and 1.09 us with 1.3 us of work among them, and for 3.4 us in the kernel before, from 1.4 us of work after a wait of 3.43 us on.
